# Two-layer graph network on one core: edges ranked in two halves, a ring of rows between the ranks and the scatters, 112-row destination blocks

## What is computed

```
msg_1 = x @ W_m1.T + b_m1
msg_2 = x @ W_m2.T + b_m2
msg_e = edge_attr @ W_me.T + b_me
msg = relu(msg_1[src] + msg_2[dst] + msg_e)          # 96 values an edge
msg = relu(msg @ W_net.T + b_net)
agg = segment_max(msg, src)                          # 0 where a node has no edge
x = layernorm(x + x @ W_o1.T + b_o1 + agg @ W_o2.T + b_o2)

message = mlp2(concat(x[src], x[dst]))               # gelu, 128 hidden
aggregated = segment_sum(message, dst)
x = layernorm(x + x + mlp2(concat(x, aggregated)))
```

## Time and profile before

| what | value |
|---|---|
| median of 3 runs | 2839.84 us (2838.89 to 2840.46) |
| profiled execution, span | 2838.6 us |
| its own time beyond the span | not recorded apart; the median is 1.2 us above the span |
| block before the ranks, with the first border groups | 0 to 194 us |
| rank-and-scatter stage (first to last scatter start) | 194.0 to 1188.0 us |
| marks and tail | to 1205 us |
| scan stage | 1207 to 1700 us |
| node stage 0 | 1700 to 1784 us |
| layer 1, edges | 1784 to 2770 us |
| node stage 1 | 2770 to 2838.6 us |
| busy: PE, DVE, POOL, ACT | 82%, 72%, 66%, 35% |

### The profile page before, as it was taken

The page is one execution under the profiler, slowest core; times in us unless marked ns, Lnnn a source line. Parts: engine busy times, 40 slices in busy tenths (PEclk is TensorE's granted clock), DMA queues, the critical chain, the costliest instruction groups (busy, mean ns, idle before and its releaser), DMA issues. The chain is left out here.

```text
span 2838.6 us, 89638 instructions
## 1 busy us (share of the span) xinstructions
PE 2320.7 (82%) x22430; PEld 2014.7 (71%) x22431; DVE 2036.0 (72%) x9631; ACT 1000.7 (35%) x2286; POOL 1860.7 (66%) x2595
## 2 busy tenths in 40 slices
PE   7778888888888888799999988876677777777777
PEld 6578777777777777477777766766677666777777
DVE  8678777777777777777787877566666666666666
ACT  7334333333333333144444447222222222222225
POOL 1047777777777777654444437677777777777774
PEclk9789999999999999899999998899999999999999
DMA  5021111111111111188888973222222222222221
GB/s 187 29 57 47 45 45 45 45 45 45 45 45 45 45 45 48 35 218 228 226 226 225 227 194 78 54 54 54 54 54 54 53 54 54 54 55 54 55 53 46
DMA packets 582003, 236.10 MB, mean 83 GB/s; under 512 B 512256, under 2 KB 553772, under 8 KB 581676
## 3 DMA queue, kind: packets, MB, share of 16 engines
q1 hardware_dynamic: 298020, 98.53, 15.3%
q0 software_dynamic: 52736, 93.92, 11.6%
q10 hardware_dynamic: 231176, 42.79, 7.5%
HBM read 142.39 MB, written 98.65 MB: 85 GB/s over the span
## 5 line engine op out<-in xcount | busy, mean ns | idle before, releaser
L1041 POOL DMA_INDIRECT edge_in_src_order<-u,place x784 | 756.6, 965 | 259.9 <-issue 185.2
L1714 POOL DMA_INDIRECT a_rows<-src_table,idx x782 | 742.2, 949 | 248.8 <-issue 237.9
L1791 PE MATMUL ps_h<-a_rows,ident 128*128 x1664 | 237.8, 286 | 247.3 <-SPq L1723 185.4
L1791 PEld LDWEIGHTS ps_h<-a_rows,ident 128*128 128x128 f32 x1664 | 202.6, 192 | 278.9 <-issue 278.7
L1411 POOL COPY m_s<-m 128x144 f32 x832 | 234.0, 325 | 244.0 <-PE ps_pre L1458 242.9
L1831 ACT ACTIVATE h<-ps_h 128x512 f32<-128x512 f32 x208 | 124.2, 597 | 743.6 <-PE ps_h L1796 653.9
L1760 DVE TENSOR_SCALAR ohd_f<-iota_b,dloc_c 128x128 f32<-128x128 bf16 x832 | 199.1, 312 | 209.8 <-PE ps_s L1805 204.1
L1434 DVE TENSOR_TENSOR_SCAN top<-same,top,ps_net 96x512 f32<-96x512 bf16 x207 | 264.1, 1276 | 97.9 <-PE ps_net L1465 97.6
L1335 ACT COPY u<-ps_u 128x384 f32<-128x384 f32 x196 | 93.7, 478 | 604.1 <-DMA edge_in_src_order<-u,place 581.7
L1258 PE MATMUL ps_u<-we_s,attrT 128*128 128x384 f32 x392 | 173.8, 525 | 158.9 <-ACT u L1335 158.9
L1748 DVE TENSOR_TENSOR hsumT<-hsumT,ps_s 128x128 f32 x832 | 238.2, 286 | 84.4 <-DVE deg L1750 1.8
(11 more groups left out here) (357 smaller groups left out, 5400.8 us busy)
## 6 DMA issues: line engine op xcount, KB each, us to landing
u_in<-edge_in_src_order SPq DMA_DIRECT2D x208, 192.0 KB, 3.4
running_max<-row ACTq DMA_DIRECT2D x208, 192.0 KB, 4.2
rowt<-src_row SPq DMA_DIRECT2D x208, 130.0 KB, 3.7
key_b<-edge_keys ACTq DMA_DIRECT2D x832, 1.5 KB
edge_in_src_order<-u,place POOLq DMA_INDIRECT x784, 2.2
a_rows<-src_table,idx POOLq DMA_INDIRECT x782
edge_attributes<-in_edge_attr SPq DMA_DIRECT2D x8, 784.0 KB, 12.0
attr_in<-edge_attributes SPq DMA_DIRECT2D x196, 32.0 KB, 1.9
```

The costliest lines, as they stand in the source:

```text
L1041: pool.indirect_dma_start(u_d, bass.IndirectOffsetOnAxis(place[:, u, j:j + 1], 0), ur[:, u, j, :], None).then_inc(sent[u], 16)
L1714: pool.indirect_dma_start(a_rows[:, 4 * u + j, :], None, a_d, bass.IndirectOffsetOnAxis(idx[:, u % 4, j:j + 1], 0)).then_inc(got[u % 4], 16)
L1791: m.matmul(ps_h[k][:, j, :], ident[:], a_rows[:].rearrange("p c d -> p (c d)")[:, bass.ds(slot[j], D)], start=(j == 0), stop=False, skip_g ...
```

## The change

It keeps the computation and changes its order and its layout in these ways.

- **Two halves.** The edges are ranked in two halves of 98 groups (`CS`), each with its own slots in src order: 444 + 444 steps, so 222 groups (`GB`) to scan instead of 208. Before the ranks only the first half's histogram is made. Between the halves (the "seam") DVE, TensorE and ACT make the second half's histogram (49 groups), its ranks, ACT's 50 splits, steps and tables, and the marks of both halves (98, with two buffers instead of four). The node stage takes the maximum of two gathered rows per node.
- **Ring.** u and the places go to rings of 40 groups (`RG`), `ring_u` and `ring_p`; copy and place of group i wait for the scatters of group i - 40. `ps_u` has two buffers. POOL's list of scatters goes on through the seam and beside the scan; the scan's first group waits for the first half's scatters, its group 111 (`GS`) for all.
- **112-row blocks.** dst blocks have 112 nodes (`BD`), and the 16 rows left hold the edge's attributes: SP loads them transposed from a scratch tensor into rows 112 to 127 of dstT, and w_e stands in the same rows of m2. The product L1258, the attribute transpose L1238 and ACT's copy L1340 go. The biases move to ACT's relu of the scan stage.
- **One-hots.** Twelve tensor_scalar and the fetch become three tensor_tensor, each for a whole group.
- **Border chain** of 14 groups (56 blocks of dst), all ahead of the ranks.
- **Zero rows.** ACT clears the second half of `running_max` with twelve DMAs of 4736 rows, at the start of its main list.
- **Staging in the scan.** POOL's four copies (f32 view, 144 wide) become two on DVE and two on ACT (bf16, 288 wide). The gathers of `agg` are issued by POOL during the scan, the first half's after group 111, the second's as `need_row` allows. Layer 1 and the last node stage are as before.

The core of the diff:

```diff
+BD = 112
+RG = 40
@@ pool
-                        pipeline(pool, CG, [(0, send)])
+                        for i in range(CG):
+                            if i == CS:
+                                pool.wait_ge(pads_set[1], 16 * NB)
+                            at, k, seen = ring_place(i, i % 4, i // 4, i // RG)
+                            wait(pool, sent[k], 64 * seen)
+                            pool.wait_ge(place_ready, i + 1)
+                            pool.wait_ge(u_ready, i + 1)
...
+                                pool.indirect_dma_start(u_d, bass.IndirectOffsetOnAxis(ring_p[:, j:j + 1], 0),
+                                                        ring_u[:, j, :], None).then_inc(sent[k], 16)
@@ vector, rank stage
-                            for j in range(4):
-                                v.tensor_scalar(ohlo[:, u, j, :], iota_b[:, 0:SL], key[:, u, 1, j:j + 1], None, ALU.is_equal)
...
+                            for table, to, size in ((lo_f, ohlo, SL), (dloc, ohd, BD), (hi_f, ohhi, HIW)):
+                                last = v.tensor_tensor(to[:, u], bcast(table[:, now].rearrange("p (c a j) -> p c a j", a=1, j=2), P, 2, size, 2),
+                                                       bcast(iota_2[:, 0:size].unsqueeze(1), P, 2, size, 2), ALU.is_equal)
@@ vector, between the halves
+                        pipeline(dve, CS, ranking, cuts=ROUNDS)
...
+                        for q in range(QS // 8):
+                            hist_onehots(dve, v, c2, ohlo_h, ohhi_h, q, 1)
+                        ranks_dve(dve, v, ch, c2, 1, bank[0], bank[1], bank[2])
...
+                        first_ranks(1, CS % 4)
+                        pipeline(dve, CG, ranking, first=CS, cuts=ROUNDS)
@@ tensor, product
-                            m.matmul(ps_u.rearrange("p j f -> p (j f)"), attrT[:, u, :], we_s[:].rearrange("p j f -> p (j f)"),
-                                     start=True, stop=False, skip_group_check=True)
@@ scalar
-                            s4, n4 = past(sent, u, n, 4)
-                            wait(act, s4, 64 * n4)
-                            s.copy(ur[:, u], ps_u).then_inc(u_ready, 1)
+                        for k in range(ZEROS):
+                            lo = POS + POS // ZEROS * k
+                            act.dma_start(s_d[lo:lo + POS // ZEROS, :].rearrange("(p s) f -> p s f", p=P),
+                                          bcast(zero_rows[:].unsqueeze(1), P, POS // ZEROS // P, F)).then_inc(rows_cleared, 16)
...
+                                act.wait_ge(sent[k], 64 * (seen - ON[k] + 1))
+                            s.copy(ring_u[:, bass.ds(4 * at, 4), :], ps_u[u % 2]).then_inc(u_ready, 1)
...
+                        def stage(i, u, n, r):
+                            wait(act, pre_ready, i - 3)
+                            at = offsets(nc, mybir.EngineType.Activation, sf_row[0:1, bass.ds(4 * i + 2, 2)], (NB - 1) * 3 * F)
+                            for j in range(2):
+                                last = s.copy(m1_s[:, u, 2 + j, :], m1[:, bass.ds(at[j], 3 * F)])
+                            last.then_inc(m1_here[1], 1)
```

More of the change, by code:

```diff
@@ L20 @@
 F32 = mybir.dt.float32
+F16 = mybir.dt.float16
 BF16 = mybir.dt.bfloat16
@@ new lines, in gnn, with hist_onehots @@
+            m2 = sb(layer0, "m2", [P, ND * F])
+            bank = [ps(layer0, f"bank{k}", [P, 512]) for k in range(8)]
+            def hist_onehots(dve, v, c, ohlo, ohhi, g, s):
+                u = g % ohlo.shape[1]
+                wait(dve, c.counted, g - ohlo.shape[1] + 1)
+                now = slice(s * QS + 8 * g, s * QS + 8 * g + 8)
+                for table, oh, size in ((lo_f, ohlo, SL), (hi_f, ohhi, NH)):
+                    last = v.tensor_tensor(oh[:, u], bcast(table[:, now].rearrange("p (c a j) -> p c a j", a=1, j=2), P, 4, size, 2),
+                                           bcast(iota_2[:, 0:size].unsqueeze(1), P, 4, size, 2), ALU.is_equal)
+                last.then_inc(c.onehots, 1)
@@ L1363, in gnn @@
[L1363 to L1374 removed]
+                marks_set = sem(t, "marks_set")
@@ new lines, in put @@
+                        def put(i, u, n, r):
+                            dve.wait_ge(place_chain, 4 * (i + 1))
+                            at, k, seen = ring_place(i, u, n, r)
+                            if not isinstance(r, int) or r > 0:
+                                dve.wait_ge(sent[k], 64 * (seen - ON[k] + 1))
+                            v.scalar_tensor_tensor(out=ring_p[:, bass.ds(4 * at, 4)], in0=across[:, u], scalar=float(MID), in1=spare[:, u],
+                                                   op0=ALU.add, op1=ALU.min).then_inc(place_ready, 1)
@@ new lines, in _ @@
+                        steps_of_c = [(2, equal), (1, turn), (3, product), (3, count)]
+                        pe.wait_ge(pick_set, 1)
+                        for k in range(CK):
+                            mm = m.matmul(ps_pick[:, 0:ND], dst_c[:, k, :], pick[:, k, :], start=(k == 0), stop=(k == CK - 1))
+                        mm.then_inc(picked, 1)
+                        for q in range(BX):
+                            border_turn(q)
+                            if q > 0:
+                                later_block(q - 1)
@@ new lines, in _, with split @@
+                        for q in range(BX):
+                            act.wait_ge(x_turned, q + 1)
+                            wait(act, x_ready, q - 1)
+                            k = min(4, ND - 1 - 4 * q)
+                            s.copy(dstT_x[:, q % 2, 0:k].rearrange("p j e -> p (j e)"), ps_split[q % 2][0:BD, 0:P * k]).then_inc(x_copied, 1)
+                        act.wait_ge(x_chain, ND)
+                        pipeline(act, CS, [(4, rows), (1, turned)], cuts=ROUNDS)
+                        def split(b):
+                            wait(act, below_ready, b - 1)
+                            s.activation(sign[:, b % 2, :], dst_f[:], ACT.Sign, scale=-1.0, bias=bounds[:, b:b + 1],
+                                         accum_out=below[:, b:b + 1]).then_inc(below_ready, 1)
```

2392 lines of the change are left out of this document (1250 added, 1142 removed).

## The result

The changed kernel takes 2867.59 us in the median of four runs (2864.14 to 2870.80), the kernel before 2839.36 us beside it: a ratio of 1.0101, 95% interval 1.0087 to 1.0116. It is slower by 1%, where 2676 us was forecast and the range ended at 2745. Its profiled execution has a span of 2866.2 us.

What follows compares the result with a forecast made beforehand. GpSimd's scatters, 1.265 us apart, were taken to bound the rank stage. 2838.6 - 216 (earlier scan start) + 49 (scan) + 3 (aggregation) = 2674.6, with 1.2 outside the span 2676 us; range 2640 to 2745.

Steps and rivals of the forecast that it cites:

- hold: Head of ScalarE's list: the twelve zero fills hold it 25 us (10 to 40); over 50 us would show it wrong.
- the border chain: Ahead of all ranks: 14 groups at 1.93 us, 27 us, and 5 for the start.
- the block before the ranks: Kernel start: half the histogram goes, 24 us saved (16 to 40), so the main block starts at 118.
- rival B: Full hold: ScalarE free only when the zero fills are nearly through, first scatter at 235; 2726 us, chance 0.20.
- The rank stage: Both halves' ranks: TensorE's turn falls from 3.95 to 3.35 us, 98 turns taking 328 us a half.
- the ring: Rank stage: group i waits for the scatter of i - 40; half 2 ends at 974 by this, 956 by ranks.
- D: Scatters slowed by DVE's new one-hots, every one 1.41 us apart; 2767 us, chance 0.06.
- D2: Seam: no scatter sends at all while DVE makes its one-hots, 89 us; 2752 us, chance 0.02.
- The seam: Between the halves: about 125 us, 49 of it for 98 marks, while GpSimd goes on sending scatters.
- The scan: Scan stage: 222 groups at 2.44 us, 542 us, +49; staging adds +0.04 a turn, shared DMA +0.03.
- Rival C: Scan: Relu, copies and TensorE's m1 products in a ring; copies of 0.5 make turns 2.65; 2723 us, chance 0.09.
- E: Zero fills: the queue passes some 240 rows a us, holding ScalarE about 240 us; 2891 us, chance 0.05.

Runs made afterwards that it cites:

- e5: The changed kernel with three zero-fill DMAs in place of twelve, the same bytes: 4062 us beside 3779 of the kernel before, at a lower TensorE clock.
- e8: The changed kernel with the zero rows cleared by one DMA of 56,832 rows in place of twelve: 2780.19 us (0.9789).
- e2: The changed kernel with VectorE's border one-hots made one group further ahead of the updates: 2838.78 us (0.9995).
- e11: The changed kernel with one fill, border one-hots further ahead, staging before relu, all m1 copies on ScalarE as f32, four mark buffers: 2674.35 us (0.9419).

## Why the prediction was wrong

Forecast and measurement between the same marks, in the profiled execution. The sum of the four differences is the whole miss, 2866.2 - 2674.6 = 191.6 us.

| stretch | forecast | measured | difference |
|---|---|---|---|
| to the first rank turn (hold, border) | 175 | 269.8 | +95 |
| ranks, seam, ranks, to the scan | 816 | 854.7 | +39 |
| scan and node stage 0 | 629 | 682.1 | +53 |
| layer 1 to the end | 1054.6 | 1059.6 | +5 |

In the first row the hold is 79 us over, the border chain 28 over, and the block before the ranks 13 under (105 against 118).

**The hold** is the largest: 104.5 us for the 25 taken, and over the 50 that the forecast named as its sign of being wrong. The step that failed is "the stall came with some eight to fourteen DMAs outstanding; at eight, four fills must land first". It made a number of DMAs out of one stalled row, whose fills were 37 times smaller and stood behind others. e5 and e8 show that an issue is held until the fill ahead of it has nearly landed. The transfer itself was undersized too: 82 us for all twelve by 267 GB/s at full share (75 of hold in rival B), where the DMA engines moved 210 GB/s at 0.93, 226 at full share, with the pad fills among them. Rival B (2726) named the mechanism and had a chance of 0.20. The Trainium skill (DMA: Bandwidth & Descriptors, Anatomy of one DMA) says of GpSimd's path that many descriptors can be emitted before it costs. On ScalarE's queue one DMA alone agrees with that, 56,832 rows issued in 0.67 us; the second in line does not.

**The border chain**: 14 x 1.93 = 27 us were forecast for a chain "unmixed". The 1.93 came from a stretch of before where VectorE's one-hots already stood ahead. The changed lists make VectorE wait for the update of the group before, 4.53 us. The order excerpt of the change did not show VectorE's loop, and I never wrote down who waits for whom across a group. e2 gives 28.8 us of it back.

**The rank stage** is right in kind and 34 us off in size (344 and 346 us for 98 turns, twice 328 forecast): the ring took away the waits, and TensorE is the bound (276.87 of 280). A turn is 3.51 us where 3.35 was taken, outside the 3.1 to 3.4 that the forecast allowed. TensorE's timeline from 400.77 to 404.32 us shows where the difference to the 3.14 lies: up to the product by m2 a turn takes 1.42 us (1.39 in the earlier trace rows without the attribute work), that product 0.93 to 1.17 in the turns around (0.86), and `more` 0.96 (0.89). These are the two products whose operands are addressed through registers; that the register loads are the cause was not tried. As forecast the scatters ran through the seam and beside the scan, and did not bound: the ring's waits are 6 us. The forecast had let the ring decide the end of half 2 (974 against 956) and added 13 us of contention and 4 to the scan's start; the ranks decided instead, the drain took some 13 us of these 35, and the 22 us left over are why the second row is 39 and not 61. Rivals D and D2 fell: the sends through the seam took 1031 ns, 7% more than the 965 of the earlier trace rows, 1.37 us apart in part of the marks and 1.26 in the rest, and were not stopped. The Trainium skill (SBUF — State Buffer, SBUF: two separate sides) has GpSimd locked out while VectorE runs two-port modes. Here 135 scatters went on beside the seam's one-hots; whether these ran in such a mode no row shows, and a lock for single instructions of 0.34 us would look like slower sends too.

**The seam**: 152 us for 125. A mark takes 0.68 us where "with two buffers instead of four 0.5" was taken, 18 us in 98. With two buffers TensorE and VectorE wait for each other in turn, and TensorE stays at its lower clock (0.50) through all the marks. The same marks in the earlier trace rows ran with four, at a clock of 0.96 to 1.00 from 1175 to 1195 us. With four the seam itself falls by 22 us (e8 against e11); the rest of the 27 was not located.

**The scan** was costed for TensorE and ScalarE: "+0.04 a turn". The step that failed is the VectorE half of the staging: the forecast saw VectorE busy 387.19 of 493 and gave it two copies without adding up its list: 1.2 + 0.24 + 0.42 + 0.38 + 0.3 of register loads is 2.5 us, above TensorE's 2.3. Rival C gave the size by luck (2.65, measured 2.64), with the wrong engine: the ring over ScalarE is worth 9 us, VectorE's copies 55. That "issue" time is not busy time hid it: VectorE is only 84% busy while it bounds.

The rival on the slower side (E, the queue's pace of 240 rows a us) is not what happened: the rows went at 56,832/104.5 = 544 a us. The time came out slower through the rows of the table together; each of them alone would have left a clear gain.

## What to carry to other kernels

Before moving work to an engine that is not the bound, add up its whole list for one turn, register loads included, and compare it with the turn; busy shares don't show it. A bulk transfer ahead of an engine's compute work should be one DMA, or stand where the engine has nothing to do: the second DMA in line holds the engine for nearly as long as the first needs. When a term has a row only from another setting (larger fills, a chain with its work already ahead, another clock), keep the far end of its range in the forecast, and let several such terms be wrong together.

## What the runs showed of the hardware

- Twelve DMAs of 4736 rows of 384 B held the issuing engine 104.5 us, three of 18,944 rows 79.6, one of 56,832 rows 0.67. With three, the second issue and the third ended 2.5 and 2.7 us before the fill ahead of them landed.
- ScalarE's relu of 96 x 512 took 683 ns with a bias of one value per partition and 592 ns without (222 and 208 instances). That it is the bias was not tried by itself.
- TensorE stayed at the lower of its two clocks (0.52 in the mean) while it was busy 108.27 of the 144 us of the seam. With four mark buffers, when it was busy 10.00 of 10 us from 583 to 593, the clock read 0.92 there, and the 98 marks took 52.2 us in place of 74.7.
